# A decoder layer's expert stage: routing weights stored expert by expert and multiplied in by VectorE

## The chip, the cores and the metric

One core of a Trainium2 chip runs the kernel. The metric is the device time of one execution in microseconds (us). TensorE is PE (its weight loads PEld), VectorE is DVE, ScalarE is ACT, GpSimd is POOL, and SP is SyncE, which here issues every DMA.

## The reference, cut to what matters

`x` is (4, 256, 128) in f32, so 1024 tokens of width 128. Three residual blocks follow one another: a self-attention in groups of 32 tokens, a cross-attention to 64 context rows with 16 heads, and a mixture of experts. Only the last matters here:

```python
scores = jax.nn.sigmoid(logits)                       # 16 experts
# the two best groups of four, then the four best experts
tw = scores of the chosen / their sum * 2.5
combine = one_hot(topk_idx) * tw, summed              # (tokens, 16)
h = jnp.einsum('td,edf->etf', x, gate_w)
u = jnp.einsum('td,edf->etf', x, up_w)
y = jnp.einsum('etf,efd->etd', silu(h) * u, down_w)   # every expert, every token
routed = jnp.einsum('etd,te->td', y, combine)
sh = silu(x @ sh_gate_w) * (x @ sh_up_w) @ sh_down_w  # two shared experts of 128
x = x + routed + sh
```

## The kernel before, in words

Everything lies in SBUF, and each engine has its own list of steps, written out by hand one after another; semaphores tie the lists together. Nothing is reordered at run time: a step that waits holds all steps behind it on its engine.

The tokens are eight tiles of 128. In the first part (to about 107 us) PE, ACT, DVE and POOL work on both attentions tile by tile, with folded weights (`fold`) computed in between. `keep_busy(n)` puts n transposes of the identity on PE. `split_hi` (L548) and `split_lo` (L553) on POOL part each expert's gate and up weights into two fp32r parts.

The expert stage works in two chunks of 512 tokens (tiles 0 to 3, then 4 to 7). For each chunk there are 18 steps: two shared experts, then 16 routed ones. So k runs over 36 steps, k = 0, 1, 18, 19 being shared. One step of the chain is:

- `gate(k)` and `up(k)` on PE, three matmuls each (lines 1629 to 1631) into one of two pairs of PSUM banks. `gate(k)` waits until `silu` of the bank's last user has read it, `up(k)` until its `multiply` has;
- `silu(k)` on ACT (L832), `multiply(k)` on DVE (L1259, one PSUM and one SBUF input), into one of four `act` buffers (tiles `s1` and `p1`, shown as s and p in the trace). `multiply(k)` waits for `down(k-4)`;
- for a routed step `weigh(k)` (on POOL, L563; the same helper exists in DVE's list but is not called): the activation times the tokens' weights for this expert, into one of three `aw` buffers (tile vbd). It waits for `multiply(k)`, for the spread transfer of this step, and for `down(k-3)`;
- `down(k)` on PE (L1671), two matmul records per step in the trace, accumulating the chunk's output in one bank.

An activation tile has the 128 hidden units on partitions and 512 tokens along the free dimension, so the weights have to lie along the free dimension and be the same in all 128 partitions. This is made so for each chunk: DVE works out `combine` (several small steps, `biased_scores` to `expert_weights`, L1140 to L1233), PE turns it (`transpose_rows`, L1620) into 64 rows of 128 tokens, row 16t + e for tile t and expert e; ACT copies these to `w_rows_sb` (`copy_rows`, L826); SP stores them to the DRAM tensor `w_rows` (`store_rows`, L394); and SP loads them back expert by expert (`load_spread`, L388), each load reading the expert's four rows of 512 B (8 KB apart, one per tile) once for each of 128 partitions, 256 KB in all. Four slots (`spread`, in the place of `wkv_sb`) hold these; a load into a used slot waits on SP for the `weigh` that reads it. `weighted(k)` gives the semaphore to wait on and `BY_VECTOR` which steps DVE weighs; it is empty.

At a chunk's end `copy_y` (ACT, L838), `turn_y` (PE, L1678) and `add_y` (DVE, L1273) add the result to x, and `store_out` (SP, L398) writes 256 KB.

Of the kernel before, what the change touches and what calls it, by code (L numbers as in the profile page):

```python
# [11 lines left out]
P = 128  # L12
# [11 lines left out]
def decoder_layer(  # L24
# [57 lines left out]
    with ExitStack() as ctx:  # L82
# [101 lines left out]
        w_rows = nc.dram_tensor("w_rows", (NCH, P // 2, P), F32, kind="Internal").ap()  # L184
# [127 lines left out]
        BY_VECTOR = ()  # L312
# [57 lines left out]
        def _(sp):  # L370
# [6 lines left out]
            def load_spread(k):  # L377
# [65 lines left out]
        def _(pool):  # L443
# [122 lines left out]
            rms(0)  # L566
            norm_scale(0, 2, 1.0, LN_EPS)
            zero_v2(0)
# [3 lines left out]
            zero_v2(2)  # L572
            norm_scale_rest()
            build_kbd(1)
            rms(2)
            build_kbd(2)
            rms(3)
            build_kbd(3)
            zero_v2(3)
            zero_v2(4)  # L580
            rms(4)
            split_hi(0)
            late_constants()
            build_kbd(4)
            zero_v2(5)
            rms(5)
            norm_scale(1, 0, 1.0 + LN_EPS, LN_EPS * LN_EPS)
            split_lo(0)
            split_hi(1)
            zero_v2(6)  # L590
            build_kbd(5)
            rms(6)
            norm_scale(1, 1, 1.0 + LN_EPS, LN_EPS * LN_EPS)
            split_lo(1)
            scale_bias()
            zero_v2(7)
            build_kbd(6)
            norm_scale(1, 2, 1.0 + LN_EPS, LN_EPS * LN_EPS)
            norm_apply(1, 0)
            norm_apply(1, 1)  # L600
            rms(7)
            build_kbd(7)
            norm_apply(1, 2)
            norm_scale(1, 3, 1.0 + LN_EPS, LN_EPS * LN_EPS)
            norm_apply(1, 3)
            norm_scale(1, 4, 1.0 + LN_EPS, LN_EPS * LN_EPS)
            norm_apply(1, 4)
            norm_scale(1, 5, 1.0 + LN_EPS, LN_EPS * LN_EPS)
            norm_p2(0)
            norm_scale(1, 6, 1.0 + LN_EPS, LN_EPS * LN_EPS)  # L610
            norm_p2(1)
            norm_apply(1, 5)
            split_hi(2)
            norm_p2(2)
            norm_scale(2, 0, 1.0, LN_EPS)
            norm_apply(2, 0)
            split_hi(3)
            split_lo(2)
            norm_apply(1, 6)
            norm_p2(3)  # L620
            norm_scale(1, 7, 1.0 + LN_EPS, LN_EPS * LN_EPS)
            norm_scale(2, 1, 1.0, LN_EPS)
            norm_apply(2, 1)
            split_hi(4)
            norm_p2(4)
            split_hi(5)
            split_hi(6)
            split_lo(3)
            norm_scale(2, 2, 1.0, LN_EPS)
            norm_apply(2, 2)  # L630
            norm_apply(1, 7)
            split_hi(7)
            norm_p2(5)
            norm_scale(2, 3, 1.0, LN_EPS)
            norm_apply(2, 3)
            split_hi(8)
            split_lo(4)
            norm_p2(6)
            split_lo(5)
            norm_scale(2, 4, 1.0, LN_EPS)  # L640
            norm_apply(2, 4)
            split_hi(9)
            split_lo(6)
# [4 lines left out]
            split_hi(10)  # L648
            norm_apply(2, 6)
            split_lo(7)  # L650
            norm_scale(2, 7, 1.0, LN_EPS)
            norm_apply(2, 7)
            split_hi(11)
            split_lo(8)
            split_lo(9)
            split_hi(12)
            split_lo(10)
            split_hi(13)
            split_lo(11)
            split_hi(14)  # L660
            split_lo(12)
            weigh(2)
            weigh(3)
            weigh(4)
            split_lo(13)
            weigh(5)
            weigh(6)
            split_hi(15)
            split_hi(16)
            split_lo(14)  # L670
            weigh(7)
            weigh(8)
            weigh(9)
            weigh(10)
            split_lo(15)
            weigh(11)
            split_hi(17)
            split_lo(16)
            weigh(12)
            split_lo(17)  # L680
            weigh(13)
            weigh(14)
            weigh(15)
            weigh(16)
            weigh(17)
            weigh(20)
            weigh(21)
            weigh(22)
            weigh(23)
            weigh(24)  # L690
            weigh(25)
            weigh(26)
            weigh(27)
            weigh(28)
            weigh(29)
            weigh(30)
            weigh(31)
            weigh(32)
            weigh(33)
            weigh(34)  # L700
            weigh(35)
        @block.scalar
        def _(sc):
# [136 lines left out]
            copy_xnT(0)  # L840
            copy_fold(("ctx", 0))
            copy_fold(("wq", 0))
            squares(0)
            copy_fold(("wq", 1))
            scale_qk(0)
            copy_qkT(0)
            copy_xnT(1)
            copy_fold(("kv", 0))
            squares(1)
            gate_tanh()  # L850
            scale_qk(1)
            copy_qkT(1)
            copy_xnT(2)
            copy_fold(("A", 0))
            squares(2)
            exp1(0)
            scale_qk(2)
            copy_p1T(0)
            copy_qkT(2)
            copy_xnT(3)  # L860
            copy_fold(("kv", 1))
            squares(3)
            copy_yT(0)
            exp1(1)
            copy_fold(("A", 1))
            scale_qk(3)
            copy_p1T(1)
            copy_qkT(3)
            copy_xnT(4)
            copy_fold(("kv", 2))  # L870
            squares(4)
            copy_yT(1)
            exp1(2)
            copy_fold(("A", 2))
            scale_qk(4)
            copy_p1T(2)
            copy_qkT(4)
            copy_xnT(5)
            copy_fold(("kv", 3))
            squares(5)  # L880
            copy_yT(2)
            exp1(3)
            scale_qk(5)
            copy_fold(("A", 3))
            copy_qkT(5)
# [1107 lines left out]
```

## Time and profile before

| | |
|---|---|
| median of 3 runs | 237.54 us (235.93 to 238.69) |
| the profiled execution | 237.24 us, its span 235.3 us |
| busy over the span | PE 200.3 us, DVE 124.4, ACT 100.8, POOL 127.7 |
| mean granted TensorE clock | 0.94 of full speed |
| DMA | 15.83 MB, mean 67 GB/s |

The time of a run holds 1.94 us around the span of the trace. A busy share is a mean over the whole span; the stages differ. The granted clock is 1.0 at full speed (2.4 GHz) and 0.5 at the lower level (1.2 GHz); a mean over a stretch may lie between.

### The profile page before, as it was taken

What the parts mean: (1) busy time and instruction counts of PE and PEld (TensorE: products, weight loads), DVE (VectorE), ACT (ScalarE), POOL (GpSimd) and SP (SyncE); (2) the same over time, 40 slices, a digit from 0 to 9 for tenths busy, and PEclk for the clock granted to TensorE, in tenths of its full rate; (3) what the DMA queues carried; (4) which work ended last, traced back from release to release, by engine and by line L of the source; (5) the groups of instructions that cost most, each with busy time, mean ns of one, the idle gap of its engine ahead of it and who ended that gap; (6) DMA issues with size and microseconds to landing.
All of it is one profiled execution on the core that took longest, in us unless ns stands there. A gap on an engine that the chain in (4) does not pass through costs nothing.

```text
span 235.3 us, 4499 instructions
## 1 busy us (share of the span) xinstructions
PE 200.3 (85%) x1597; PEld 136.1 (58%) x1597; DVE 124.4 (53%) x271; ACT 100.8 (43%) x241; POOL 127.7 (54%) x207
## 2 busy tenths in 40 slices
PE   6688899989999999999998259987999789497952
PEld 5456566666678777777857115645676356264611
DVE  4824578575698877888796014597322213023211
ACT  2364888978577644557754011321222213122200
POOL 5366355983514899787684158648620260264560
PEclk9979999999999999999999857997999958979998
DMA  5850000000510840000001453743302504555421
GB/s 122 314 150 0 3 6 4 3 3 0 149 36 0 249 110 0 1 3 0 0 4 19 93 104 82 119 116 96 91 9 33 126 22 68 110 103 136 108 57 45
DMA packets 28983, 15.83 MB, mean 67 GB/s; under 512 B 1681, under 2 KB 28706, under 8 KB 28834
## 3 DMA queue, kind: packets, MB, share of 16 engines
q1 hardware_dynamic: 28962, 15.56, 26.9%
q8 instruction: 13, 0.21, 0.4%
q14 instruction: 8, 0.07, 0.1%
HBM read 14.96 MB, written 0.59 MB: 66 GB/s over the span
## 4 chain that ended last, share of the span: by engine, by line
PE 45%; DMA 34%; ACT 5%; DVE 5%; issue 4%; SPq 3%; POOL 2%; POOLq 1%; DVEq 0%; ACTq 0%
DMA wkv_sb<-w_rows 30%; PE bank L1599 7%; PE wide L1570 6%; PE bank L1547 3%; PE bank L1671 3%; PE bank L1555 3%; PE bank L1584 3%; PE bank L1540 2%; PE wide L1629 2%; PE wide L1631 2%; PE wide L1630 2%; DMA wq_sb<-in_L_xattn_w_q_dram 2%; DMA w_rows<-w_rows_sb 2%; PE bank L1597 1%; PE bank L1455 1%
## 5 line engine op out<-in xcount | busy, mean ns | idle before, releaser
L832 ACT ACTIVATE kbd<-wide 128x512 f32<-128x512 f32 x36 | 21.5, 598 | 78.0 <-PE wide L1631 39.6
L1629 PE MATMUL wide<-x3hi,gu_lo 128*128 128x512 f32 x72 | 41.5, 577 | 2.9 <-POOL gu_lo L553 2.5
L563 POOL TENSOR_TENSOR vbd<-s,wkv_sb 128x512 f32<-128x512 f32 x16 | 20.4, 1277 | 36.2 <-DMA wkv_sb<-w_rows 28.6
L1671 PE MATMUL bank<-vbd,wq_sb 128*128 128x512 f32 x32 | 21.6, 776 | 13.4 <-POOL vbd L563 13.2
L563 POOL TENSOR_TENSOR vbd<-p,wkv_sb 128x512 f32<-128x512 f32 x16 | 20.3, 1274 | 21.4 <-DMA wkv_sb<-w_rows 15.4
L1259 DVE TENSOR_TENSOR p<-kbd,wide 128x512 f32<-128x512 f32 x18 | 12.3, 685 | 36.0 <-PE bank L1671 20.4
L1630 PE MATMUL wide<-x3lo,gu_hi 128*128 128x512 f32 x72 | 30.1, 418 | 0.0
L1631 PE MATMUL wide<-x3hi,gu_hi 128*128 128x512 f32 x72 | 30.0, 417 | 0.0
L1259 DVE TENSOR_TENSOR s<-kbd,wide 128x512 f32<-128x512 f32 x18 | 12.3, 684 | 29.7 <-PE bank L1671 17.6
L1629 PEld LDWEIGHTS wide<-x3hi,gu_lo 128*128 128x128 f32 x72 | 14.6, 203 | 13.4 <-issue 7.6
L1671 PE MATMUL bank<-vbd,wqT 128*128 128x512 f32 x32 | 17.3, 624 | 4.0 <-POOL vbd L563 3.9
L457 POOL TENSOR_TENSOR p<-p,rs 128x1024 f32<-128x1024 f32 x8 | 15.3, 1911 | 7.6 <-DVE rs L1101 7.6
L1630 PEld LDWEIGHTS wide<-x3lo,gu_hi 128*128 128x128 f32 x72 | 14.5, 201 | 8.3 <-issue 6.4
L1671 PEld LDWEIGHTS bank<-vbd,wq_sb 128*128 128x128 f32 x32 | 6.8, 236 | 20.3 <-POOL vbd L563 13.7
L1599 PE MATMUL bank<-vo_fold,p2T 128*128 128x128 f32 x128 | 17.2, 281 | 0.0
L1631 PEld LDWEIGHTS wide<-x3hi,gu_hi 128*128 128x128 f32 x72 | 14.5, 202 | 3.6
L1599 PEld LDWEIGHTS bank<-vo_fold,p2T 128*128 128x128 f32 x128 | 15.4, 191 | 1.1
L1570 PE MATMUL wide<-qk_fold,xn2T 128*128 128x512 f32 x32 | 15.1, 593 | 0.0
L517 POOL TENSOR_TENSOR kbd<-qkT,hmask 128x512 f32<-128x512 f32 x8 | 8.8, 1096 | 8.8 <-ACT qkT L737 8.8
L1088 DVE TENSOR_REDUCE mx<-wide 128x16 f32<-128x1024 f32 x8 | 9.7, 1216 | 3.8 <-PE wide L1570 3.6
L553 POOL TENSOR_TENSOR gu_lo<-v,gu_hi 128x256 fp32r<-128x256 f32 x16 | 11.6, 730 | 0.0
L1671 PEld LDWEIGHTS bank<-vbd,wqT 128*128 128x128 f32 x32 | 5.9, 197 | 8.9 <-POOL vbd L563 7.3
(157 smaller groups left out, 404.6 us busy)
## 6 DMA issues: line engine op xcount, KB each, us to landing
wkv_sb<-w_rows SPq DMA_DIRECT2D x32, 256.0 KB, 8.1
wkv_sb<-in_L_xattn_w_kv_dram SPq DMA_DIRECT2D x1, 1024.0 KB, 6.9
v<-in_L_ffn_gate_w_dram SPq DMA_DIRECT2D x4, 256.0 KB, 4.4
v<-in_L_ffn_up_w_dram SPq DMA_DIRECT2D x4, 256.0 KB, 5.8
wq_sb<-in_L_xattn_w_q_dram SPq DMA_DIRECT2D x1, 512.0 KB, 4.5
wout_sb<-in_L_xattn_w_out_dram SPq DMA_DIRECT2D x1, 512.0 KB, 6.1
wq_sb<-in_L_ffn_down_w_dram SPq DMA_DIRECT2D x1, 512.0 KB, 3.8
wqT<-in_L_ffn_down_w_dram SPq DMA_DIRECT2D x1, 512.0 KB, 5.5
```

The costliest lines, as they stand in the source:

```text
L457: pool.tensor_tensor(p2[:, t % 3, :, :], p2[:, t % 3, :, :], rs2[:, t % 2, :].unsqueeze(2).to_broadcast([P, H2, CTX]), ALU.mult).then_inc( ...
L553: pool.tensor_tensor(gu_lo[:, n, :, :], gu_of(n), gu_hi[:, n, :, :].bitcast(F32), ALU.subtract).then_inc(wsplit_lo, 1)
L563: pool.tensor_tensor(aw[k % 3], act[k % 4], spread[:, r % SPREAD, :, :].rearrange("p t q -> p (t q)"), ALU.mult).then_inc(awp_s, 1)
L832: sc.activation(sil[:, k % 2, :], bank[up_bank(k)], ACT.Silu).then_inc(sil_s, 1)
L1088: dve.tensor_reduce(mx2[:, t % 2, :], s, AX.X, ALU.max).then_inc(mx2_s, 1)
L1259: dve.tensor_tensor(act[k % 4], sil[:, k % 2, :], bank[up_bank(k) + 1], ALU.mult).then_inc(g_s, 1)
L1570: last = pe.matmul(wide[:, scores_bank(t) + n, :], xn2T[:, t % 2, :], fold_b[:, n * 512:(n + 1) * 512], start=True, stop=True)
L1599: last = pe.matmul(OUT2[:, 0:D], p2T[:, j, :], vo_fold[:, j, b, :], start=False, stop=(j == NPAIR - 1))
L1629: pe.matmul(dst, lo, x3hi[:, cols], start=True, stop=False)
L1630: pe.matmul(dst, hi, x3lo[:, cols], start=False, stop=False)
L1631: return pe.matmul(dst, hi, x3hi[:, cols], start=False, stop=True)
L1671: pe.matmul((FOLD, PV)[c], dn_of(n), rhs, start=(n == 0), stop=(n == NE - 1)).then_inc(y_s, 1)
```

## The change

The DRAM tensor gets one contiguous row of 4 × 128 weights for each expert, so that a spread transfer reads one piece of 2 KB for each partition. The store of a chunk becomes four DMAs, one per tile. All 32 routed steps are weighed by DVE, none by POOL. And the order of the steps in all four engines' lists is written anew.

```diff
-        w_rows = nc.dram_tensor("w_rows", (NCH, P // 2, P), F32, kind="Internal").ap()
+        w_rows = nc.dram_tensor("w_rows", (NCH, E, TPC, P), F32, kind="Internal").ap()
...
-        BY_VECTOR = ()
+        BY_VECTOR = range(NK)
...
                 if e == 0:
-                    sp.wait_ge(rows_st, 16 * (c + 1))
+                    sp.wait_ge(rows_st, 16 * TPC * (c + 1))
...
                 sp.dma_start(spread[:, r % SPREAD, :, :],
-                             w_rows[c].rearrange("(t e) q -> e t q", e=E)[e].partition_broadcast(P)
-                             ).then_inc(sp_l[r % SPREAD], 16)
+                             w_rows[c, e].partition_broadcast(P)).then_inc(sp_l[r % SPREAD], 16)
...
                 sp.wait_ge(rows_s, c + 1)
-                sp.dma_start(w_rows[c], w_rows_sb[0:TPC * E, c, :]).then_inc(rows_st, 16)
+                for t in range(TPC):
+                    sp.dma_start(w_rows[c, :, t, :], w_rows_sb[E * t:E * (t + 1), c, :]).then_inc(rows_st, 16)
```

POOL's list loses its 32 `weigh` calls, so the last `split_lo` and `split_hi` follow one another. Of DVE's new list, chunk 0's start, the seam of the chunks, and the end:

```diff
+            chosen_scores(0)
+            expert_weights(0)
+            multiply(2)
...
+            multiply(5)
+            biased_scores(1)
+            weigh(2)
+            weigh(3)
+            weigh(4)
             multiply(6)
...
+            weigh(16)
+            weigh(17)
+            expert_weights(1)
             multiply(18)
             multiply(19)
             multiply(20)
             multiply(21)
             multiply(22)
+            weigh(20)
+            weigh(21)
+            weigh(22)
+            add_y(0)
             multiply(23)
+            weigh(23)
...
             multiply(35)
+            weigh(34)
+            weigh(35)
             add_y(1)
```

PE's new order, in words with `g`, `u`, `d` for gate, up and down. Start: `keep_busy(14)`, `keep_busy(10)`, then tile 0's first transpose (before, the 10 stood behind `scores1(0)`). Around the first rows: `transpose_rows(0)` d1 u3 u4 g5 g6 u5 g7 u6 g8 g9 u7 d2 (before: d1 u3 `transpose_rows(0)` u4 g5 g6 u5 g7 u6 g8 u7 g9 d2). Around the second: g20 g21 u19 d15 `transpose_rows(1)` d16 d17 u20 g22 u21 g23 u22 d18 u23 `turn_y(0)` u24 d19 g24 d20 (before, `transpose_rows(1)` stood ahead of d12, and 8 downs, 7 gates and 9 ups lay between it and d20). In ACT's list `copy_rows(0)` stands before `silu(3)` instead of behind it, `copy_rows(1)` behind `silu(21)` instead of ahead of it. In the attention part the folds of context weights (`("kv", j)`, `("A", j)`) come one tile earlier on PE and ACT, and the scores of the cross-attention (`scores2`) somewhat later.

## Rows read from the trace of the kernel before

**Rows 1.** The page: the chain that ended last, shares of the span by line

```profile
DMA wkv_sb<-w_rows 30%; PE bank L1599 7%; PE wide L1570 6%; PE bank L1547 3%; PE bank L1671 3%; PE bank L1555 3%; PE bank L1584 3%; PE bank L1540 2%; PE wide L1629 2%; PE wide L1631 2%; PE wide L1630 2%; DMA wq_sb<-in_L_xattn_w_q_dram 2%; DMA w_rows<-w_rows_sb 2%; PE bank L1597 1%; PE bank L1455 1%
```

**Rows 2.** Windows: us, PE, PEld, DVE, ACT, POOL busy, clock, DMA share, GB/s

```profile
172.00:185.00 13.00, 13.00 (x51) 8.96 (x50) 4.12 (x6) 3.68 (x8) 1.10 (x2) 1.00 0.21 43
185.00:190.00 5.00, 2.21 (x5) 0.80 (x5) 0.69 (x1) 0.00 (x0) 2.68 (x3) 0.87 0.40 105
```

**Rows 3.** Timeline of the first rows and weights, all engines

```profile
124.12 0.30 PE L1620 MATMUL bank<-ident,combine 128*64 128x128 f32 x1 [1.01 <-DVE combine L1233]
124.74 0.52 SPq L394 DMA_DIRECT2D w_rows<-w_rows_sb  x1
126.58 37.38 SPq L388 DMA_DIRECT2D wkv_sb<-w_rows  x16
134.50 1.26 POOL L563 TENSOR_TENSOR vbd<-p,wkv_sb 128x512 f32<-128x512 f32 x1 [8.56 <-DMA wkv_sb<-w_rows]
135.91 2.04 PE L1671 MATMUL bank<-vbd,wq_sb 128*128 128x512 f32 x2 [5.14 <-POOL vbd L563]
```

**Rows 4.** Groups between 124 and 236 us: line, count, busy, mean ns, idle before

```profile
L1629 PE MATMUL wide<-x3hi,gu_lo 128*128 128x512 f32 x63 | 37.0, 587 | 2.5 <-POOL gu_lo L553 2.5
L1671 PE MATMUL bank<-vbd,wq_sb 128*128 128x512 f32 x32 | 21.6, 776 | 13.4 <-POOL vbd L563 13.2
L563 POOL TENSOR_TENSOR vbd<-s,wkv_sb 128x512 f32<-128x512 f32 x16 | 20.4, 1277 | 36.2 <-DMA wkv_sb<-w_rows 28.6 <-DVE s L1259 4.3 <-PE bank L1671 1.9
L563 POOL TENSOR_TENSOR vbd<-p,wkv_sb 128x512 f32<-128x512 f32 x16 | 20.3, 1274 | 21.4 <-DMA wkv_sb<-w_rows 15.4 <-PE bank L1671 2.7 <-DVE s L1259 1.8
L1671 PE MATMUL bank<-vbd,wqT 128*128 128x512 f32 x32 | 17.3, 624 | 4.0 <-POOL vbd L563 3.9
L553 POOL TENSOR_TENSOR gu_lo<-v,gu_hi 128x256 fp32r<-128x256 f32 x7 | 5.1, 731 | 0.0
```

**Rows 5.** Chain at full clock: start, us on the chain, what

```profile
167.62 0.86 PE bank L1671 x2
168.48 0.23 PE wide L1629
168.71 0.23 PE wide L1630
168.94 0.24 PE wide L1631
```

**Rows 6.** Chain at the end of the span

```profile
220.38 7.53 DMA wkv_sb<-w_rows
...
230.53 0.59 ACT y_sb L838
```

**Rows 7.** Issue to landing: spread loads (L388), gate weights (L428), row stores (L394)

```profile
DMA to landing us min/median/max: 7.5/8.1/13.1
...
DMA to landing us min/median/max: 2.7/4.4/5.6
...
DMA to landing us min/median/max: 1.8/1.8/1.8
```

**Rows 8.** Windows (columns as in rows 2): gate loads, then weight rows

```profile
77.00:79.00 2.00, 1.87 (x13) 1.30 (x11) 1.97 (x3) 0.98 (x2) 2.00 (x2) 1.00 0.94 279
178.00:182.00 4.00, 4.00 (x15) 2.59 (x14) 0.86 (x2) 0.60 (x1) 0.00 (x0) 1.00 0.27 42
183.00:186.00 3.00, 2.46 (x14) 1.71 (x12) 0.69 (x1) 1.44 (x3) 1.28 (x1) 1.00 0.59 153
```

**Rows 9.** Timeline: a DVE step with SBUF inputs alone, and one beside POOL

```profile
18.57 0.69 DVE L1064 TENSOR_TENSOR s<-s,mx 128x512 f32<-128x512 f32 x1
...
154.12 1.27 POOL L563 TENSOR_TENSOR vbd<-p,wkv_sb 128x512 f32<-128x512 f32 x1 [1.35 <-issue]
154.13 1.34 DVE L1193 TENSOR_TENSOR r_a<-r_a,r_g 128x64 f32<-128x64 f32 x1
```

**Rows 10.** Timeline of PE: the ten keep-busy transposes

```profile
16.75 1.92 PE L1439 MATMUL bank<-ident 128*128 128x128 f32 x10
```

More of the change, by code:

```diff
@@ L975, in _ @@
             exp_logits(7)
+            copy_rows(0)
             silu(3)
-            copy_rows(0)
             silu(4)
@@ L994, in _ @@
             silu(20)
+            silu(21)
             copy_rows(1)
-            silu(21)
             silu(22)
+            copy_y(0)
             silu(23)
-            copy_y(0)
             silu(24)
@@ L1284, in _ @@
             norm_stats(0, 4)
-            norm_apply(0, 1)
             norm_stats(0, 5)
@@ L1400, in _ @@
+            rank_groups(1)
             multiply(10)
+            weigh(8)
+            weigh(9)
+            weigh(10)
             multiply(11)
-            rank_groups(1)
+            multiply(12)
+            weigh(11)
             mask_groups(1)
-            multiply(12)
+            weigh(12)
+            split_x3(7)
+            multiply(13)
+            weigh(13)
+            multiply(14)
+            multiply(15)
             choose_experts(1)
-            multiply(13)
-            split_x3(7)
+            multiply(16)
@@ L1408, in _ @@
             chosen_scores(1)
-            multiply(14)
+            weigh(14)
+            weigh(15)
+            multiply(17)
+            weigh(16)
+            weigh(17)
             expert_weights(1)
-            multiply(15)
-            multiply(16)
-            multiply(17)
             multiply(18)
@@ L1874, in _ @@
             gate(8)
+            gate(9)
             up(7)
-            gate(9)
             down(2)
@@ L1879, in _ @@
             down(4)
+            gate(10)
             up(8)
             up(9)
+            gate(11)
             down(5)
-            gate(10)
+            gate(12)
             up(10)
+            down(6)
+            gate(13)
             up(11)
-            down(6)
-            gate(11)
             down(7)
-            gate(12)
-            gate(13)
             up(12)
-            up(13)
             down(8)
             gate(14)
+            up(13)
+            gate(15)
+            gate(16)
             down(9)
-            gate(15)
             down(10)
-            gate(16)
             up(14)
+            down(11)
             up(15)
-            down(11)
+            down(12)
             up(16)
-            transpose_rows(1)
-            down(12)
             gate(17)
-            down(13)
             up(17)
             gate(18)
+            up(18)
+            down(13)
+            gate(19)
             down(14)
-            gate(19)
+            gate(20)
+            gate(21)
+            up(19)
             down(15)
-            up(18)
-            up(19)
-            gate(20)
+            transpose_rows(1)
+            down(16)
+            down(17)
             up(20)
-            down(16)
-            gate(21)
+            gate(22)
             up(21)
-            down(17)
+            gate(23)
             up(22)
@@ L1922, in _ @@
             up(23)
-            gate(22)
+            turn_y(0)
+            up(24)
             down(19)
-            gate(23)
-            up(24)
             gate(24)
-            turn_y(0)
+            down(20)
+            gate(25)
+            gate(26)
+            down(21)
+            down(22)
             up(25)
-            down(20)
-            down(21)
-            gate(25)
+            down(23)
+            gate(27)
             up(26)
-            down(22)
-            gate(26)
-            gate(27)
-            down(23)
             gate(28)
+            gate(29)
             up(27)
-            gate(29)
-            gate(30)
             up(28)
             down(24)
+            gate(30)
             up(29)
-            gate(31)
+            up(30)
             down(25)
             down(26)
-            up(30)
+            gate(31)
             gate(32)
@@ L1951, in _ @@
             gate(33)
+            down(27)
             up(32)
-            down(27)
             down(28)
+            gate(34)
             down(29)
+            gate(35)
             up(33)
+            up(34)
             down(30)
-            gate(34)
-            gate(35)
-            up(34)
+            up(35)
             down(31)
-            up(35)
             down(32)
```

467 lines of the change are left out of this document (223 added, 244 removed).

## The prediction
> **What bounds the kernel now.** I read four views in this order. The page's chain first: the spread loads of the weight rows are 30% of the chain that ended last, by far its largest line [rows 1]. All of it lies behind 126 us, so the expert stage is where the end is set, and in it a transfer, not an engine. Then windows: where PE has work it is busy all the time at full clock, and where weights are awaited it is busy 2.21 us of 5 and the clock falls [rows 2]. Then the timeline of the first weights: the rows are turned at 124.12, stored at 124.74, the first load is issued at 126.58, POOL can weigh only at 134.50, and PE, out of gate and up matmuls at 130.77, stands idle 5.14 us until the first routed down at 135.91 [rows 3]. Last the groups of the stage: POOL's 32 weighs wait 28.6 and 15.4 us for transfers, and PE's downs wait 13.4 and 4.0 us for POOL [rows 4].
>
> How far down could the stage go? At full clock one product (gate or up) takes 0.23 + 0.23 + 0.24 = 0.70 us of PE's chain and one down 0.86 [rows 5]. From 124.12 on 63 products are left (three groups of 63 matmuls) [rows 4] and 34 downs (36 less the first two): 63 × 0.70 + 34 × 0.86 = 44.1 + 29.2 = 73.3 us, and 0.6 for two row transposes and the first turn of y. PE would be done at 198.0. In fact the last down ends at 230.5 [rows 6]. So 32.5 us of the stage are PE's waits (13.4 + 4.0 + 2.5 = 19.9 us in rows 4) and the slow clock that follows them (the rest). That is the most that this change can win here.
>
> **Why the loads are slow, and what 2 KB pieces do.** One load moves 0.262 MB in 512 pieces of 512 B. The gate weights are loaded in transfers of the same size and the same pieces; they ran at 279 GB/s, a load of the weight rows that is alone in flight at 42 GB/s, and four in flight at 153 once the first is through [rows 8]. So neither the piece size nor the number of pieces can be the whole reason: what differs is the source. Every partition reads the same four places, 8 KB apart. My reading: a place of the DRAM gives some 42 GB/s, the four rows at a stride of 8 KB count as one such place, and different experts, 512 B apart, as different ones. 0.262 MB at 42 GB/s is 6.2 us, plus the 1.8 us that even the small store takes, is 8.0; the median landing is 8.1 [rows 7]. With the four pieces side by side the load would reach over the distances that now lie between experts, so one load should get what four get now: 0.262 / 153 = 1.7, plus 1.8, is 3.5 us. The bounds: 2.7 us, the fastest gate load, and 8.1, nothing gained [rows 7]; beyond it the third rival. I take 3.5, because the rate of four in flight is the nearest row to "several places at once".
>
> The Trainium skill, "Perfetto Trace Analysis", section "DMA Optimizations", says that DMAs under 2 KB carry a large overhead and that making them larger is the first thing to do. The gate loads with pieces of 512 B at 279 GB/s speak against that as the cause; by it the load would come to the same 2.7 to 3.5 us, by another way.
>
> **Part by part.**
> - *First weights.* In the new lists `expert_weights(0)` stands before `multiply(2)`, and the down and the product d1 and u3 behind the row transpose; I take `combine` 1 us earlier (0 to 2). The store is four DMAs instead of one: three more issues on SP of about 0.5 us, as the first took 0.52 [rows 3], so +1.5 us, with nothing else queued on SP. The load lands 3.5 us after its issue instead of 7.9 (126.58 to 134.50): −4.4. The weigh takes DVE 0.69 us, as a step of the same shape with SBUF inputs does, not 1.28 [rows 4, 9]: −0.6. The first routed down starts at 135.9 − 1 + 1.5 − 4.4 − 0.6 = 131.4 against PE's end of work at 130.8 − 1: a wait of 1.6 us instead of 5.1, too short, I think, for the clock to fall.
> - *Steady part.* PE needs 2 × 0.70 + 0.86 = 2.26 us for one k. DVE now needs 0.69 + 0.69 = 1.38, ACT 0.60, as its copy of the same size does [rows 6, 9]. Four slots turn in 3.5 + 0.4 (issue) + 0.7 (weigh) + about 1 of waiting = 5.6 us, or 1.4 per load. So PE is the bound, and both the transfers and DVE lie beside it. If the load stayed at 8.1 the slots would turn in 10.2, 2.55 per load, above PE's 2.26: then the cover is gone. DVE is a single list: a `weigh` that waits for its load also holds the multiplies behind it, and these free PSUM banks. For such small waits I put 0.1 us per down, 3.4 in all (0 to 10).
> - *Seam.* PE's second row transpose waits for `expert_weights(1)`, which stands behind `weigh(17)` on DVE: 1 us (0 to 3). From there: two multiplies, one silu and the copy itself to the end of `copy_rows(1)` (it stands behind `silu(21)`, which waits for `multiply(19)`), 1.4 + 0.6 + 0.3 = 2.3 us, four stores 1.5 + 1.8, the load 3.5, the weigh 0.7, is 9.8 us. PE has in the list up to d20: four downs, eight products less one, the turn of y, 3.4 + 4.9 + 0.5 = 8.8, and some waits between; a wait of about 1 us. Before, the list had much more work there, but the weights came so late that PE was idle still [rows 2].
> - *POOL.* Without weighs its last splits no longer stand behind a transfer; PE's wait of 2.5 us for `gu_lo` goes [rows 4] (it is within the 32.5).
> - *Ports.* DVE's step with two SBUF inputs at 154.13 took 1.34 us, though it has 64 elements per partition and the 0.69 us step 512, while POOL's weigh ran from 154.12 to 155.39 [rows 9]. After the change POOL has only splits of 0.73 us [rows 4] beside DVE's weighs; ten of them could hold DVE at most 7 us, of which DVE's spare 0.9 us per k takes nearly all. The Trainium skill, "SBUF — State Buffer", section "Who interferes with whom", calls the pair of ports that the two share an exclusive lock. By that rule, the trace agrees with 1.34 us; it speaks against a move to DVE only while POOL still works.
> - *Attention part.* The ten keep-busy transposes, 1.92 us on the chain at 16.75 [rows 10], go to the front, where PE would otherwise wait for its first input. The new order of folds and scores I can't price closely; PE is nearly full from 60 us on either way. I take −1 us (−3 to +3).
> - *End.* From the last down to the end of the span 4.8 us [rows 6], unchanged.
>
> **The sum.** Span 235.3 − 32.5 + 1.6 + 1 + 1 + 3.4 − 1 = 208.8. With the 1.94 us around the span 210.7. The profiled execution stands 0.3 us under the median of the runs shown, which is within their spread. I round to 210.5 us. Its own range is 202 (no small waits, load 2.7) to 221 (load at 5, each start of a chunk 2 us later and a slow clock behind).
>
> **The rivals.**
> - *The load stays as slow (8.1 us), as each transfer still reads from one place.* For it: 2 KB is small beside the 8 KB over which the four rows lay, and the reads of all partitions still meet. Against it: 153 GB/s with neighbouring experts in flight. First down: 135.9 − 1 + 1.5 − 0.6 = 135.8, as before. Slots: −0.6 / 4 = −0.15 per load over 24 loads, −3.6. Seam: weights after 14.4 us, PE's work 8.8 to 9.8, some 2 us more idle than now. Splits −2.5, attention −1. Sum −5: 232 us (228 to 239). This is also the case that the change doesn't do what it says.
> - *Slower: DVE's list is held by late loads.* The load stays at 8.1, and now a weigh that waits stops the multiplies behind it, so PE loses gate and up work that it now does in the meantime. POOL waits 28.6 us for transfers in one group and 15.4 in the other, 44 us [rows 4]; PE is idle 19.9; so about 24 us of these waits are covered by such work. If half of that cover goes, 232 + 12 = 244 us. It decides against the change once over 5 of the 24 us go, and only if the load stays above 7 us. Against it: `multiply(k)` waits for `down(k-4)` anyway, so PE can't run far ahead even now.
> - *Slower: the 2 KB are one place, and loads no longer overlap.* Then each costs 6.2 us, where now 32 take 101.3 us, seam included (126.6 to 227.9) [rows 3, 6], 3.2 each. That is the break-even; in full it gives 237 + 32 × 3.0 = 333 us. For it only that the source is narrower than before; against it the four different experts in flight, which stay.
>
> **How the numbers follow.** Likeliest 0.71; load unchanged 0.13; DVE held 0.11; no overlap 0.05. A measurement of this kernel can tell about 1% from no change. Faster by over 1%: 0.71 + 0.09 of the second case = 0.80; within 1%: 0.04; slower 0.11 + 0.05, and nothing of the second case's 239 to speak of = 0.16. The range reaches from 202 over the second case to 236; what is left out are the two slower rivals, 0.16, and a little below.
>
> **What would show it.** Right: median landing of the spread loads near 3.5 us with its rate above 100 GB/s alone in flight; PE's idle time before downs under 5 us in all; the clock at 1.0 from 124 us on; weighs of 0.69 us on DVE; the chain of the stage made of PE lines. The prediction is wrong if the landing stays near 8 us, or if it falls and PE still waits more than 10 us for DVE's weighs, or if the part up to the first row transpose moves by over 3 us.

## The result and the profile after

The changed kernel takes 205.96 us (205.46 to 206.56, 4 runs) against 237.44 (235.93 to 238.69) for the kernel before on the same chip: ratio 0.868 [0.862, 0.873], 31.5 us faster. Some executions of a kernel come out 1.5% or more slower than its others; medians and ranges below leave them out, and the traces of e1, e7 and e11 are of such executions. The profiled execution took 205.46 us with a span of 203.4 (before 235.3) and a mean granted clock of 0.987. The forecast was 210.5 us, from 202 to 236.

The page of the profile of the kernel after: its clock in 40 slices, the chain by engine and by line, and the spread loads (count, size, us to landing).

```profile
PEclk9988999999999999999999999999999999999998
...
PE 65%; POOL 11%; ACT 8%; DVE 5%; issue 3%; DMA 3%; SPq 2%; POOLq 0%; ACTq 0%
PE bank L1671 13%; PE wide L1629 6%; PE wide L1631 6%; PE wide L1630 6%; PE wide L1570 6%; PE bank L1599 6%; POOL gu_lo L553 5%; PE bank L1547 4%; PE bank L1540 3%; DMA beta_col<-in_L_xattn_ln_beta_dram 3%; POOL gu_hi L548 3%; ACT k L742 3%; ACT v L742 3%; PE bank L1584 2%; PE bank L1555 2%
...
wkv_sb<-w_rows SPq DMA_DIRECT2D x32, 256.0 KB, 3.3
```

Against [rows 1] the spread load, 30% of the chain, has gone from it altogether. The three lines of a product and the downs (L1629 to L1631, L1671) are 31% and now set most of the end: the stage has become a stage of PE, but for its start. There the chain runs through POOL's splits (`gu_lo` 5% and `gu_hi` 3%) until 133.29 us. The median landing fell from 8.1 us [rows 7] to 3.3.

Windows of the kernel after (columns as in rows 2): the first loads in flight, a load alone in flight, then the first loads of the second chunk.

```profile
125.00:129.00 4.00, 4.00 (x18) 3.00 (x16) 3.21 (x5) 1.16 (x2) 4.00 (x7) 1.00 0.81 260
139.50:141.00 1.50, 1.50 (x7) 1.13 (x6) 1.50 (x4) 0.60 (x1) 0.00 (x0) 1.00 0.47 158
160.00:170.00 10.00, 10.00 (x39) 6.64 (x37) 5.05 (x8) 2.92 (x6) 0.00 (x0) 1.00 0.35 108
165.00:169.00 4.00, 4.00 (x17) 2.63 (x16) 2.07 (x4) 0.20 (x1) 0.00 (x0) 1.00 0.83 262
```

These answer to [rows 2, 8]. A load alone now gets 158 GB/s at its height where it got 42, and several together 260 where they got 153; PE is busy all 10 us around the seam, where it had been busy 2.21 of 5.

Groups of the kernel after from 124 us on (line, count, busy, mean ns, idle before).

```profile
L1629 PE MATMUL wide<-x3hi,gu_lo 128*128 128x512 f32 x61 | 32.6, 534 | 0.3 <-POOL gu_lo L553 0.3
L1671 PE MATMUL bank<-vbd,wq_sb 128*128 128x512 f32 x32 | 16.2, 601 | 0.6 <-DVE vbd L1235 0.6
L1671 PE MATMUL bank<-vbd,wqT 128*128 128x512 f32 x32 | 15.5, 593 | 0.0
L1235 DVE TENSOR_TENSOR vbd<-p,wkv_sb 128x512 f32<-128x512 f32 x16 | 11.7, 754 | 0.4 <-PE bank L1671 0.4
L1235 DVE TENSOR_TENSOR vbd<-s,wkv_sb 128x512 f32<-128x512 f32 x16 | 11.4, 720 | 3.2 <-PE bank L1671 2.2 <-DMA wkv_sb<-w_rows 1.0
```

Set beside [rows 4]: PE's three waits of 13.4, 4.0 and 2.5 us are 0.6, 0 and 0.3. The 44 us that the weighs waited for transfers are 1.0. A weigh is 0.72 to 0.75 us instead of 1.28.

### The profile page after: what moved, and what is told of

Same layout as the page of the kernel before. It is cut to its first block, busy times and chain, and to the rows that moved or that the text cites. A ratio compares the mean times of both kernels' runs of the same rounds, so it can differ in the third digit from the quotient of the medians.

```text
span 203.4 us, 4505 instructions
## 1 busy us (share of the span) xinstructions
PE 188.0 (92%) x1597; PEld 132.0 (65%) x1597; DVE 140.1 (69%) x303; ACT 100.2 (49%) x241; POOL 90.3 (44%) x175
## 2 busy tenths in 40 slices
DMA packets 16791, 15.83 MB, mean 78 GB/s; under 512 B 1777, under 2 KB 12418, under 8 KB 16642
## 4 chain that ended last, share of the span: by engine, by line
PE 65%; POOL 11%; ACT 8%; DVE 5%; issue 3%; DMA 3%; SPq 2%; POOLq 0%; ACTq 0%
PE bank L1671 13%; PE wide L1629 6%; PE wide L1631 6%; PE wide L1630 6%; PE wide L1570 6%; PE bank L1599 6%; POOL gu_lo L553 5%; PE bank L1547 4%; PE bank L1540 3%; DMA beta_col<-in_L_xattn_ln_beta_dram 3%; POOL gu_hi L548 3%; ACT k L742 3%; ACT v L742 3%; PE bank L1584 2%; PE bank L1555 2%
## 5 line engine op out<-in xcount | busy, mean ns | idle before, releaser
L1629 PE MATMUL wide<-x3hi,gu_lo 128*128 128x512 f32 x72 | 38.1, 529 | 0.3 <-POOL gu_lo L553 0.3
L1631 PE MATMUL wide<-x3hi,gu_hi 128*128 128x512 f32 x72 | 28.6, 397 | 0.0
L1630 PE MATMUL wide<-x3lo,gu_hi 128*128 128x512 f32 x72 | 28.5, 395 | 0.0
L1227 DVE TENSOR_TENSOR s<-kbd,wide 128x512 f32<-128x512 f32 x18 | 12.3, 684 | 11.4 <-PE wide L1631 5.7
L1629 PEld LDWEIGHTS wide<-x3hi,gu_lo 128*128 128x128 f32 x72 | 13.6, 189 | 8.8 <-issue 5.9
L1227 DVE TENSOR_TENSOR p<-kbd,wide 128x512 f32<-128x512 f32 x18 | 12.3, 684 | 9.9 <-PE bank L1671 5.8
L1671 PE MATMUL bank<-vbd,wq_sb 128*128 128x512 f32 x32 | 16.2, 601 | 0.6 <-DVE vbd L1235 0.6
L517 POOL TENSOR_TENSOR kbd<-qkT,hmask 128x512 f32<-128x512 f32 x8 | 10.0, 1256 | 13.3 <-ACT qkT L705 13.2
L1631 PEld LDWEIGHTS wide<-x3hi,gu_hi 128*128 128x128 f32 x72 | 13.5, 188 | 3.2
L1671 PE MATMUL bank<-vbd,wqT 128*128 128x512 f32 x32 | 15.5, 593 | 0.0
L1235 DVE TENSOR_TENSOR vbd<-s,wkv_sb 128x512 f32<-128x512 f32 x16 | 11.4, 720 | 3.2 <-PE bank L1671 2.2
L772 ACT COPY p2T<-bank 128x512 f32<-128x512 f32 x16 | 9.2, 578 | 6.7 <-PE bank L1584 6.7
L1547 PE MATMUL bank<-k,wqT 128*128 128x256 f32 x32 | 9.4, 402 | 2.8 <-ACT v L742 2.7
L1235 DVE TENSOR_TENSOR vbd<-p,wkv_sb 128x512 f32<-128x512 f32 x16 | 11.7, 754 | 0.4 <-PE bank L1671 0.4
```

The costliest lines, as they stand in the source:

```text
L1227: dve.tensor_tensor(act[k % 4], sil[:, k % 2, :], bank[up_bank(k) + 1], ALU.mult).then_inc(g_s, 1)
L1235: dve.tensor_tensor(aw[k % 3], act[k % 4], spread[:, r % SPREAD, :, :].rearrange("p t q -> p (t q)"), ALU.mult).then_inc(awv_s, 1)
L1547: last = pe.matmul(FOLD[:, m * B * CTX:(m + 1) * B * CTX], wqT[:, j, :], k2[:, j % 2, bs, :, :].rearrange("p b h s -> p (b h s)"), start=T ...
L1629: pe.matmul(dst, lo, x3hi[:, cols], start=True, stop=False)
L1630: pe.matmul(dst, hi, x3lo[:, cols], start=False, stop=False)
L1631: return pe.matmul(dst, hi, x3hi[:, cols], start=False, stop=True)
```

## The experiments

The change has three parts: the layout of the rows in memory, the engine that weighs, and the order of the lists. My theory was that the layout brings nearly all, and through where the rows lie, not through the size of a piece. The rivals: the piece size does it; the engine or the order does it.

### Where the gain comes from

**e1_rows8k**: the kernel after with the rows 8 KB apart again, in pieces of 512 B.

```diff
-w_rows = nc.dram_tensor("w_rows", (NCH, E, TPC, P), ...)
+w_rows = nc.dram_tensor("w_rows", (NCH, TPC, E, P), ...)
-    sp.dma_start(w_rows[c, :, t, :], ...)
+    sp.dma_start(w_rows[c, t, :, :], ...)
-    w_rows[c, e].partition_broadcast(P)
+    w_rows[c, :, e, :].partition_broadcast(P)
```

> The kernel after, with only the DRAM layout undone: an expert's four rows lie 8 KB apart again and a load reads pieces of 512 B; four stores, VectorE's weighs and the new order stay. If the layout carries the gain, the loads land in about 8 us again and the time is 229 to 245 us. The two rivals of the prediction part here: if only the slot loop counts, about 232 us; if VectorE's list is held by the late loads and products stop with it, about 244 us. If the order and VectorE carried the gain, the time would stay below 212 us even with loads of 8 us.

Measured: 230.33 us (229.13 to 230.4), ratio to before 0.974 [0.967, 0.980]; landings of 7.4, 8.5 and 12.0 us (min, median, max). The layout is worth 24.4 us here.

**e2_layout_only**: the kernel before, with the layout alone; POOL weighs, old order.

```diff
-w_rows = nc.dram_tensor("w_rows", (NCH, P // 2, P), ...)
+w_rows = nc.dram_tensor("w_rows", (NCH, E, TPC, P), ...)
-    sp.wait_ge(rows_st, 16 * (c + 1))
+    sp.wait_ge(rows_st, 16 * TPC * (c + 1))
-    w_rows[c].rearrange("(t e) q -> e t q", e=E)[e].partition_broadcast(P)
+    w_rows[c, e].partition_broadcast(P)
-    sp.dma_start(w_rows[c], w_rows_sb[0:TPC * E, c, :])
+    for t in range(TPC):
+        sp.dma_start(w_rows[c, :, t, :], w_rows_sb[E * t:E * (t + 1), c, :])
```

> The kernel before, with only the new DRAM layout and its four stores; GpSimd weighs, the old order stays. If the layout carries the gain: loads land in 3 to 3.5 us, the waits for transfers go, and what is left is GpSimd's splits and weighs in one list and the attention part as before; 212 to 218 us. If the order and the move to VectorE carry most of it, the time stays above 225 us.

Measured: 214.61 us (214.25 to 214.89), ratio 0.909 [0.904, 0.913]; landing 3.3 us. The layout alone brings 22.8 of the 31.5 us (9.1% of the time by the ratio to the kernel before on its own chip, which is 21.6 us).

**e3_pool_weighs**: the kernel after, its layout and order kept, with the weighs on POOL between and behind its splits.

```diff
-BY_VECTOR = range(NK)
+BY_VECTOR = ()
 # vector list: every weigh(k) goes
 # POOL's list, behind split_lo(12) ... split_lo(17):
+weigh(2) ... weigh(17), weigh(20) ... weigh(35)
```

> The kernel after, with its layout and its order, but GpSimd weighs all 32 routed steps again (in its list the weighs stand among the last splits as in the kernel before), and VectorE none. If the move to VectorE matters only by 0.6 us in the two starts of a chunk: 206 to 208 us. If GpSimd's list (weighs behind splits, splits behind weighs) matters: 209 to 213 us, with TensorE waiting for gu_lo or for the weigh near 130 us.

Measured: 207.31 us (206.88 to 208.15), ratio 0.880 [0.872, 0.887], so 1.4 us over the kernel after, with intervals that touch. A group of its weighs from 122 us on, with the PE groups of the products and of the downs behind the weighs:

```profile
L1629 PE MATMUL wide<-x3hi,gu_lo 128*128 128x512 f32 x64 | 34.4, 538 | 2.2 <-DVE s L1259 1.1 <-POOL gu_lo L553 0.5 <-ACT kbd L832 0.5
L563 POOL TENSOR_TENSOR vbd<-s,wkv_sb 128x512 f32<-128x512 f32 x16 | 20.6, 1295 | 20.5 <-PE bank L1671 11.1 <-DMA wkv_sb<-w_rows 9.2
L1671 PE MATMUL bank<-vbd,wq_sb 128*128 128x512 f32 x32 | 16.0, 598 | 0.1
```

POOL takes 1.30 us for the one weigh of each k, PE needs 2.26 us for that k, and PE waits 0.1 us for the weighs; in e2, with the old order, it waits 2.5 us for them where it had waited 17.4. So POOL wasn't the bound of this stage: its lateness in the kernel before was that of the transfers which it waited for.

**e12_pool_8k**: e3's kernel with e1's layout, to see whether late loads hurt more in DVE's list than in POOL's.

```diff
 # e3_pool_weighs
-w_rows = nc.dram_tensor("w_rows", (NCH, E, TPC, P), ...)
+w_rows = nc.dram_tensor("w_rows", (NCH, TPC, E, P), ...)
 # store and load as in e1_rows8k
```

> The kernel after with two parts undone: an expert's four rows 8 KB apart, and GpSimd's weighs (the list of the run with GpSimd's weighs in the new order). Against the run with the rows 8 KB apart and VectorE's weighs (230.4 us) it shows what VectorE's list costs when loads are late. If late loads held by VectorE's list cost products, as the slower rival says, this one is faster, 222 to 228 us. If multiply(k) waits for down(k-4) anyway, or GpSimd's longer weigh costs as much, it is 230 to 234 us.

Measured: 231.04 us (230.49 to 231.3), ratio 0.974 [0.968, 0.981]. With slow loads DVE (230.33) and POOL (231.04) come out alike. The waits for transfers and those of PE's products, us, count and longest, are in e1 and in e12:

```profile
DVE vbd L1235 <- DMA wkv_sb<-w_rows: 23.1, 10, 5.0
PE wide L1629 <- DVE p L1227: 6.5, 3, 4.3
```

```profile
POOL vbd L563 <- DMA wkv_sb<-w_rows: 35.2, 13, 12.0
PE wide L1629 <- POOL gu_lo L553: 3.6, 2, 2.7
PE wide L1629 <- DVE s L1259: 0.8, 1, 0.8
```

DVE's list does stand still for 23.1 us, as the second rival said, and PE's products do wait for the multiplies behind it, 6.5 us in e1's trace against 0.8 in e12's. But POOL's list is held in the same way: in e12 its late weighs hold the splits behind them, and the products wait 3.6 us for `gu_lo`. The two costs nearly cancel, so the equal times don't show that late loads cost DVE's list nothing.

The four kernels and the two of the case make a table (us), in which the layout and the order stand clear of the intervals and the engine doesn't. The kernels ran on several chips, on which the kernel before took 236.05 to 237.44 us, so about 1 us of any difference is no finding:

| | rows 8 KB apart | expert by expert | layout |
|---|---|---|---|
| old order, POOL weighs | 237.44 | 214.61 | -22.8 |
| new order, POOL weighs | 231.04 | 207.31 | -23.7 |
| new order, DVE weighs | 230.33 | 205.96 | -24.4 |
| order | -6.4 | -7.3 | |
| engine | -0.7 | -1.4 | |

The traces divide the order's share. The first row transpose starts at 124.12 us in the kernel before and 126.22 in e2, at 120.81 in e12 and 121.26 in e3. Less the 1.56 us of one product and one down that the new order puts behind it, the attention part won 1.8 us in the one pair and 3.4 in the other. From there to the last down PE's waits and slow stretches, by the count of products and downs, fell by 4.3 and 3.8 us.

### Piece size or place

The theory of places gives a number for each pitch: with 42 GB/s per place [rows 8], the rate is bounded by the place that serves the largest share of the reads. These four kernels are the kernel after with another shape of `w_rows`; all read pieces of 512 B. Each was run once.

```diff
 # e5_pitch1k; 8 * P in e9_4k, 16 * P in e10_all8k
-w_rows = nc.dram_tensor("w_rows", (NCH, E, TPC, P), ...)
+w_rows = nc.dram_tensor("w_rows", (NCH, E, TPC, 2 * P), ...)
 # in words:
-    store to w_rows[c, :, t, :], load from w_rows[c, e]
+    store to w_rows[c, :, t, 0:P], load from w_rows[c, e, :, 0:P]
 # e4_pitch17
-w_rows = nc.dram_tensor("w_rows", (NCH, E, TPC, P), ...)
+w_rows = nc.dram_tensor("w_rows", (NCH, TPC, E + 1, P), ...)
 # in words:
+    store to w_rows[c, t, 0:E, :], load from w_rows[c, :, e, :]
```

**e5_pitch1k** (rows 1 KB apart):

> The kernel after, with every row of 512 B in its own 1 KB: pieces of 512 B, the four of an expert 1 KB apart, within 4 KB. Theory of places: near neighbours are different places, loads land in 3 to 4 us, time 206 to 209 us. Theory of piece size: about 8 us again. If this one is fast and the distance of 8704 B slow, a place is wider than 1 KB but the four rows must lie close together, and neither theory holds as it stands.

**e4_pitch17** (rows 8704 B apart, that is 8 KB and 512 B):

> The kernel after, but with an expert's four rows of 512 B at a distance of 8704 B (17 rows for a tile instead of 16), so the pieces are as small as before and only the distance differs from 8192 B. Theory of places (a stride of 8 KB makes the four rows one place of the DRAM): loads land in 3 to 4 us, time about 206 to 209 us. Theory of piece size (small pieces are slow from a shared source): loads land in about 8 us, time as with the old layout.

**e9_4k** (every row at a multiple of 4 KB):

> The kernel after, with every row of 512 B alone in 4 KB, so an expert's four rows lie 4 KB apart and those of all experts at multiples of 4096 B. If places repeat every 8 KB only, the rows are two places, a load gets 80 to 90 GB/s and lands in about 5 us, several in flight get no more than that, 3 us for each load, and the time is 225 to 240 us. If they repeat every 4 KB: as with 8 KB, 328 us. If the distance must be a multiple of 8 KB to hurt at all: 206 to 209 us.

**e10_all8k** (every row at a multiple of 8 KB, all experts too):

> The kernel after, with every row of 512 B alone in 8 KB, so that not only an expert's four rows but those of all 16 experts lie at multiples of 8192 B. Theory of places: different experts are now one place too, so loads in flight no longer help one another; the rate stays at 40 to 45 GB/s however many are in flight, a load costs 6 us, the stage some 200 us, and the time is 300 to 340 us. If the slowness comes from an expert's own four rows only, it is as with the old layout: 230 us, with bursts of 150 GB/s.

Windows, first of e1 while its first load is moved, then of e4, e5, e9 and e10 with several loads in flight (columns as in rows 2; the last is GB/s):

```profile
126.00:130.00 4.00, 3.71 (x16) 2.64 (x15) 2.64 (x4) 0.75 (x2) 4.00 (x7) 1.00 0.24 43
```

```profile
125.00:129.00 4.00, 4.00 (x18) 3.01 (x17) 3.15 (x5) 1.20 (x2) 4.00 (x7) 1.00 0.54 154
```

```profile
125.00:129.00 4.00, 4.00 (x18) 3.20 (x18) 2.92 (x5) 1.34 (x3) 4.00 (x7) 1.00 0.79 225
```

```profile
140.00:160.00 20.00, 13.25 (x39) 7.93 (x39) 8.74 (x21) 2.59 (x5) 0.00 (x0) 0.84 1.00 77
```

```profile
130.00:160.00 30.00, 12.31 (x26) 5.66 (x26) 7.57 (x16) 1.79 (x3) 2.04 (x4) 0.72 0.42 40
240.00:300.00 60.00, 33.83 (x77) 18.92 (x77) 12.80 (x20) 5.98 (x10) 0.00 (x0) 0.73 0.61 47
```

| kernel | piece, distance of an expert's four rows | median landing, us | GB/s | time, us |
|---|---|---|---|---|
| after | 2 KB in one | 3.3 | 260 | 205.96 |
| e5 | 512 B, 1 KB | 3.6 | 225 | 205.71 (one run) |
| e4 | 512 B, 8704 B | 4.5 | 154 | 205.64 (one run) |
| e1 | 512 B, 8 KB, experts 512 B apart | 8.5 | 43, then 85 to 128 | 230.33 |
| e9 | 512 B, 4 KB, experts 16 KB apart | 12.3 | 70 to 77 | 250.68 (one run) |
| e10 | 512 B, 8 KB, experts 32 KB apart | 21.2 | 40 to 47 | 328.03 (one run) |

The size of a piece is the same from e5 to e10, and the landing goes from 3.6 to 21.2 us. So it is the distance that costs, where all partitions read the same rows. The gate weights show that this condition belongs to it: their load (`gate_w[es].rearrange("e d f -> d e f")`) gives each partition four pieces of 512 B that lie 64 KB apart, and runs at 279 GB/s [rows 8], but the rows of neighbouring partitions are 512 B apart, so that all partitions together don't meet in one place.

With everything at multiples of 8 KB 40 to 47 GB/s is all there is, however many loads are in flight, as if one place served all. At multiples of 4 KB the theory has two places, 84 GB/s by 2 × 42, and 77 were seen at a DMA share of 1.00, so a busy DMA engine here is not one that moves much. What a place is in the chip no run shows: the theory is a count that fits, not a part that was seen. The 512 B added to the 8 KB in e4 are enough to win the whole time back, since 4.5 us is still below what PE's pace needs.

The theory is rough in places. e9's rate came out a little under the 80 to 90 GB/s expected, its median landing at 12.3 us where 5 was expected (5.5 is its shortest), and its time 11 us above the range; about 3 us of that time may be a held step of DVE that is no matter of the layout (last section). e4's loads landed in 4.5 us, not 3 to 4. And e4 and e5 read four rows at different offsets of 8 KB both, yet give 154 and 225 GB/s. Counted over four loads in flight, the offset used most serves 4 of 16 rows in e4 (at most 42 × 16 / 4 = 168 GB/s) and 2 of 16 in e5; that would fit, but no run tests it.

The Trainium skill, "Perfetto Trace Analysis", section "DMA Optimizations", puts a significant overhead on DMAs under 2 KB. Each load here is one DMA of 256 KB, so the rule is applied to its pieces. With the rows 1 KB apart a load in pieces of 512 B lands in 3.6 us against 3.3 in pieces of 2 KB. So piece size costs at most 0.3 us per load here, and no time; whoever follows the rule meets the cure, by its side effect on the places.

### The rest: stores, keep-busy and the ports

**e6_one_store**: `combine` written expert by expert, so that one store of 32 KB takes the place of four.

```diff
-combine = sb("combine", [P, NT, E])
+combine = sb("combine", [P, NCH, E, TPC])
 ...   # expert_weights, transpose_rows and the wait of load_spread to match
-    for t in range(TPC):
-        sp.dma_start(w_rows[c, :, t, :], ...)
+    sp.dma_start(w_rows[c].rearrange("e t q -> (e t) q"), w_rows_sb[0:TPC * E, c, :])
```

> The kernel after, with VectorE writing combine expert by expert, so that the row transpose gives the rows in the order of the DRAM layout and one DMA stores them instead of four. Both theories agree that the first load is issued about 0.9 to 1.4 us earlier. If TensorE's wait of 0.6 us before the first routed down is all that this can win: 205 to 206 us. If it moves more (VectorE's weighs come earlier than GpSimd's splits allow), up to 1.5 us less; if writing with a stride costs, no gain.

Measured: 205.53 us (204.63 to 205.74), ratio 0.871 [0.862, 0.879]: no difference that can be measured. Timeline of the kernel after, then of e6:

```profile
120.67 0.27 PE L1620 MATMUL bank<-ident,combine 128*64 128x128 f32 x1
121.27 1.73 SPq L394 DMA_DIRECT2D w_rows<-w_rows_sb  x4
...
127.75 0.68 DVE L1112 TENSOR_TENSOR biased<-score,rowb 128x64 f32<-128x64 f32 x1
...
128.31 3.00 POOL L553 TENSOR_TENSOR gu_lo<-v,gu_hi 128x256 fp32r<-128x256 f32 x3
128.35 2.37 DVE L1235 TENSOR_TENSOR vbd<-p,wkv_sb 128x512 f32<-128x512 f32 x2
...
129.74 3.30 PE L1671 MATMUL bank<-vbd,wq_sb 128*128 128x512 f32 x6 [0.61 <-DVE vbd L1235]
```

```profile
120.39 0.52 SPq L393 DMA_DIRECT2D w_rows<-w_rows_sb  x1
122.22 7.99 SPq L388 DMA_DIRECT2D wkv_sb<-w_rows  x6
...
127.50 2.37 DVE L1234 TENSOR_TENSOR vbd<-p,wkv_sb 128x512 f32<-128x512 f32 x2
```

The first load of the kernel after is issued at 124.04, 3.37 us behind the row transpose; in e6, where the transpose starts at 119.80, it is 2.42 us. The saved 0.95 us buys nothing: in both kernels the first weigh starts where DVE comes out of the routing step before it (127.75 + 0.68 in the kernel after), and PE's wait is 0.6 us in both.

**e7_keep_busy_back** moves the ten keep-busy transposes back behind `scores1(0)`; **e11_no_extra** removes them.

```diff
 keep_busy(14)
-keep_busy(10)
 ...
 scores1(0)
+keep_busy(10)   # e7 only
```

> The kernel after, with the ten keep-busy transposes put back behind the first scores of the self-attention. If these 1.9 us are what the attention part won, the first row transpose comes at 122 to 122.5 us instead of 120.6 and the time is 207 to 208 us. If they are hidden there as they were on the chain before by chance only, or if the rest of the new order won it, the time stays at 205.5 to 206.5 us.

> The kernel after without the ten keep-busy transposes that stand in front (fourteen stay). If they lie in time in which TensorE waits for its first input: 205.5 to 206.5 us, with the first row transpose at 120.6 as now. If they delay that input's transpose: up to 1.5 us less. If they hold the clock up for the first matmuls: up to 1.5 us more, with a lower granted clock in the first 20 us.

Measured: e7 207.1 us (206.68 to 208.16), ratio 0.877 [0.866, 0.888], and e11 206.42 (205.86 to 207.06), 0.871 [0.864, 0.878]. The first row transposes start at 121.93 and 122.18 against 120.67. But in ten traces of kernels with the same attention part, the kernel after among them, this start goes from 119.80 to 121.28. The clock of the first 20 us in the two is 0.83 against 0.91 in the kernel after, and e3, which has all the transposes in front, shows 0.83 too. Both medians lie above that of the kernel after, but the intervals overlap its own, so what the transposes are worth stays open between nothing and about 1 us. The order's 6 to 7 us sit mostly elsewhere in it; which of its other moves wins them wasn't taken apart.

**e8_pool_beside**: 32 spare multiplies of 128x512 behind POOL's last split, work which the output doesn't need, to see what DVE pays beside a working POOL.

```diff
 split_lo(17)
+pool.memset(idle_a[:, :], 1.0)
+for n in range(32):
+    pool.tensor_tensor(idle_b[:, :], idle_a[:, :], idle_a[:, :], ALU.mult)
+    ...   # each waits for the one before
```

> The kernel after, and behind GpSimd's last split 32 multiplies of 128x512 from one spare buffer into another, one behind the other, which the output doesn't need. If the two engines exclude one another while both read two SBUF inputs, VectorE's weighs beside them take up to 1.3 us more each; TensorE needs 2.26 us for a step and VectorE then up to 2.7, so over the 14 or so weighs of the 41 us it loses 3 to 8 us: 209 to 214 us. If they do not, the weighs stay at 0.69 us and the time at 205.5 to 206.5 us.

Measured: 217.95 us (216.88 to 218.42), ratio 0.919 [0.912, 0.925], 12 us over the kernel after, and 4 over the top of what I expected. Groups of e8 from 122 us on, then its timeline:

```profile
L676 POOL TENSOR_TENSOR idle_b<-idle_a 128x512 f32<-128x512 f32 x32 | 37.4, 1168 | 2.5
L1243 DVE TENSOR_TENSOR vbd<-p,wkv_sb 128x512 f32<-128x512 f32 x16 | 15.6, 992 | 0.1
L1243 DVE TENSOR_TENSOR vbd<-s,wkv_sb 128x512 f32<-128x512 f32 x16 | 13.6, 858 | 0.7 <-DMA wkv_sb<-w_rows 0.6
L1235 DVE TENSOR_TENSOR p<-kbd,wide 128x512 f32<-128x512 f32 x17 | 11.5, 682 | 8.9 <-PE bank L1679 4.7 <-ACT kbd L808 3.1 <-PE wide L1639 1.0
```

```profile
141.72 0.21 DVE L1149 TENSOR_TENSOR cmp_a<-r_g 128x64 f32<-128x64 f32 x1
...
142.96 1.08 DVE L1154 TENSOR_TENSOR cmp_a<-cmp_a,cmp_b 128x64 f32<-128x64 f32 x1
```

The weighs go from 754 and 720 ns to 992 and 858 on average. Small routing steps stretch as well: the one at 142.96 takes 1.08 us for 64 elements, about the 1.17 of one POOL multiply, where the same step takes 0.23 in the kernel after with POOL idle; but the one at 141.72 got through in 0.21. The multiplies of the chain, which take one input from PSUM, keep their 0.68 us (L1235). DVE is then full (15.83 of 16 us in the window from 134 to 150) and PE busy only 11.79 of them.

## Why the prediction was right

**The bound and the mechanism.** That the stage could fall nearly to PE's own floor of 73.9 us from the row transpose on was right. In the kernel after, the last down ends at 198.65, by the chain (start, us on the chain, what):

```profile
194.31 4.34 PE bank L1671 x10
198.65 0.02 issue
198.67 0.59 ACT y_sb L806
```

From 120.67 that is 78.0 us. PE's work in it is one product and one down more than before: 64 × 0.70 + 35 × 0.86 + 0.6 = 75.5. So all that is lost together is 2.5 us, and the end (4.7 us from there) is the 4.8 that were forecast.

**The load.** 3.5 us forecast, 3.3 measured; e1, e4, e9 and e10 show that the distance between the rows costs, as the reading by places had it, and e5 takes away the size of a piece. The rate taken for a load alone, 153 GB/s, was near too: 158 were seen from 139.50 to 141.00, and 260 only with several in flight.

**First weights.** The first row transpose comes 3.45 us earlier, 1.9 by count, as 1.56 us of work now stand behind it; the sum had 1 for the attention part. The prediction named a move of this part by over 3 us as a sign of being wrong, and by the trace that sign was met. It doesn't touch the mechanism, since nearly half of it is the work moved, which the sign left out; but the gain of the attention part was too small in the forecast. Stores: 0.9 us more from transpose to first load (3.37 against 2.46), not 1.5, and e6 shows that even they are covered. The weigh was forecast at 0.69 us and took 1.2 beside POOL's splits (2.37 for two), which themselves took 1.0 (3.00 for three) instead of 0.73: what the part on ports expected, but on both sides. The Trainium skill, "SBUF — State Buffer", section "Who interferes with whom", calls the shared pair of ports an exclusive lock; the trace agrees, with 1.2 against 0.69 us. PE waited 0.6 us at the first down, not 1.6. But the next two downs, of 0.86 us each, stood behind weighs of 1.2, and the product behind them waited for the last split. The chain there, then PE's timeline:

```profile
128.35 2.97 POOL gu_lo L553 x3
131.31 1.02 POOL gu_hi L548
132.37 0.89 POOLq L82
133.29 0.47 PE wide L1629
```

```profile
133.29 0.47 PE L1629 MATMUL wide<-x3hi,gu_lo 128*128 128x512 f32 x1 [0.25 <-POOL gu_lo L553]
```

From 120.67 to 133.29 PE has ten products, four downs and a transpose, 10.5 us of work in 12.6: 2.1 us are lost here, where the sum had 1.6.

**Steady part, seam and small waits: the term that was mis-sized.** I put 3.4 us on waits of 0.1 us per down, 1 on the seam and 1 on the second row transpose, 5.4 in all. From 133.29 to the last down's end at 198.65 PE has 54 products, 31 downs, a transpose and a turn, 65.0 us of work in 65.4: these terms measured 0.4 together. The seam cost nothing: transpose at 159.63, loads from 164.22, weigh(20) at 167.62, its down at 169.30, and PE busy throughout (the window from 160 to 170). So 7.0 in the sum (1.6 + 5.4) were 2.5, nearly all of it at the first weights. These 4.5 us and the 0.9 of the row transpose are the 5.4 between the forecast span of 208.8 and 203.4. Nothing in [rows 4] spoke for 0.1 us per down; it was put in as prudence and should have been left out, with DVE's spare 0.9 us in every 2.26.

**The rivals.** The load that stays slow was set up in e1: 230.3 us, against 232 forecast, so the price was right and the condition wrong. DVE held by late loads costs nothing over POOL held by them (230.33 against e12's 231.04). The effect that the rival named is there, 6.5 us of waiting products in e1's trace, but it takes the place of another of POOL's and never came near the 12 us priced for it. The loads that no longer overlap were set up in e10: 328.03 us, against 333 forecast, when all experts' rows lie at multiples of 8 KB. In the change itself the experts lie 2 KB apart and don't.

**What I gave no price.** The new order of the lists is worth 6.4 to 7.3 us by the table, the second largest part: 1.8 to 3.4 in the attention part, the rest fewer waits of PE in the stage. I had it at 1 (attention) + 1 (earlier `combine`), with the rest inside PE's waits. Since the total rests on PE's floor and not on the parts, this did no harm to the sum, which is luck as far as the parts go; a forecast of the parts would have missed.

## What to carry to other kernels

When many partitions read one small buffer, look at the distance between the rows that are read together before the size of a piece: at 8 KB a load of 256 KB took 8.5 us and at 1 KB 3.6, with the same pieces. Rows 64 KB apart did no harm where each partition read its own. A low DMA rate with a full DMA share (77 GB/s at 1.00) or a rate that doesn't grow with loads in flight (40 to 47) pointed to the source here. Where a stage can be brought down to one engine's work, sum that engine's work from the last fixed event to the end and add only waits that a row shows.

## What was not expected of the hardware

**Padding of 512 B is enough.** 8704 B instead of 8192 between the rows takes the rate from 43 to 154 GB/s and the kernel from 230.3 to 205.6 us (one run).

**A working POOL stretches small steps of DVE too.** 1.08 us against 0.23 for the same 64 elements; with the weighs it came to 12 us over the stage.

**One small DVE step of 4.7 us.** In e11's profiled execution, timeline of DVE and PE, then of POOL:

```profile
127.86 4.68 DVE L1108 TENSOR_SCALAR r_a<-eneg 128x64 f32<-128x64 f32 x1
...
134.14 3.65 PE L1671 MATMUL bank<-vbd,wq_sb 128*128 128x512 f32 x4 [3.48 <-DVE vbd L1235]
```

```profile
127.86 1.43 POOL L553 TENSOR_TENSOR gu_lo<-v,gu_hi 128x256 fp32r<-128x256 f32 x2
129.26 0.61 POOL L548 TENSOR_TENSOR gu_hi<-v,zero_col 128x256 fp32r<-128x256 f32 x1
129.83 2.09 POOL L553 TENSOR_TENSOR gu_lo<-v,gu_hi 128x256 fp32r<-128x256 f32 x3
131.88 0.61 POOL L548 TENSOR_TENSOR gu_hi<-v,zero_col 128x256 fp32r<-128x256 f32 x1
132.57 0.72 POOL L553 TENSOR_TENSOR gu_lo<-v,gu_hi 128x256 fp32r<-128x256 f32 x1
```

The same step takes 0.80 us at 126.33 in the kernel after. PE lost 3.48 us to it at the first routed down, and this execution took 210.57 us where the others of e11 took 205.86 to 207.06. It is no single case: the step takes 4.71 us in e7's trace, 4.74 in e9's and 4.72 in e10's. In all four POOL's splits run one behind the other while it lasts, each at its short time (0.70 to 0.72 us for `gu_lo`), and the step ends within 0.1 us of the first gap between them (here POOL stops at 132.49 and goes on at 132.57, and the step ends at 132.54). So it looks as if POOL's whole train of splits held it. What decides whether it is held stays open: in the six other traces with DVE's weighs in the new order, the kernel after among them, the splits start within 0.03 us of the step as well, and it takes about 0.8 us.
